# The first attention unit's scores and group maxima, moved from the attention stage into the value loop of the projection

## The reference

```
x = LN(x + attention(x));  x = LN(x + softmax(cross scores) * ...);  x = LN(x + mixture_of_experts(x))
```

```
q, k, v = x@Wq+bq, x@Wk+bk, x@Wv+bv          # split into 16 heads of 32
local:   query block i (128 rows) sees keys in [128 i - 64, 128 (i+1) + 64)
global:  row 0, row 511 and the 62 rows of largest |q| per head see all 512 keys
```

## Time and profile before

| | us |
|---|---|
| three executions | 1150.06, 1471.1, 1154.42 |
| median | 1154.42 |
| profiled execution | 1150.03 |
| its span, first to last instruction | 1148.3 |

### The profile page before, as it was taken

The page is one execution under the profiler, slowest core; times in us unless marked ns, Lnnn a source line. Parts: engine busy times, 40 slices in busy tenths (PEclk is TensorE's granted clock), DMA queues, the critical chain, the costliest instruction groups (busy, mean ns, idle before and its releaser), DMA issues. The chain is left out here.

```text
span 1148.3 us, 18035 instructions
## 1 busy us (share of the span) xinstructions
PE 983.3 (86%) x5111; PEld 710.3 (62%) x5111; DVE 761.1 (66%) x1328; ACT 612.8 (53%) x919; POOL 465.8 (41%) x423
## 2 busy tenths in 40 slices
PE   5999995899999999971899999992879999999940
PEld 4567884434444344420798989891868888888830
DVE  3325534877777677603888888853777888888925
ACT  4333210366767667642444444441667888888824
POOL 2000000154546455445566666623234555555424
PEclk9999998699999999985899999996899999999975
DMA  7454404443424334004211111123785444344327
GB/s 253 152 183 165 165 1 83 82 102 65 110 65 99 88 76 109 1 1 163 63 56 56 57 55 55 56 66 129 254 254 135 73 72 73 72 73 73 65 37 293
DMA packets 80881, 115.71 MB, mean 101 GB/s; under 512 B 15680, under 2 KB 37056, under 8 KB 80832
## 3 DMA queue, kind: packets, MB, share of 16 engines
q1 hardware_dynamic: 65648, 90.17, 27.0%
q0 software_dynamic: 9760, 20.49, 9.8%
q10 hardware_dynamic: 5424, 4.46, 1.2%
HBM read 74.77 MB, written 40.31 MB: 100 GB/s over the span
## 5 line engine op out<-in xcount | busy, mean ns | idle before, releaser
L718 DVE TENSOR_REDUCE maxima<-ps_s 128x8 f32<-128x512 f32 x256 | 168.7, 689 | 71.1 <-PE ps_s L586 69.4
L554 POOL TENSOR_TENSOR pair_sum<-probs 128x2048 f32<-128x2048 f32 x32 | 146.0, 4564 | 164.1 <-ACT probs L693 164.1
L1643 DVE TENSOR_TENSOR we_lo<-w_all,we_hi 128x1408 fp32r<-128x1408 f32 (+1 forms) x117 | 188.7, 1666 | 29.8 <-ACT we_hi L1583 24.4
L693 ACT ACTIVATE probs<-ps_st 128x512 f32<-128x512 f32 x256 | 146.4, 600 | 93.2 <-PE ps_st L635 89.6
L1583 ACT ACTIVATE we_hi<-w_all 128x1408 fp32r (+1 forms) x117 | 161.4, 1412 | 34.6 <-PE e_ps_y L1691 15.3
L586 PE MATMUL ps_s<-k,q 96*128 96x512 f32 x256 | 115.2, 458 | 14.9 <-DMA k<-qk_dram 11.9
L635 PE MATMUL ps_st<-q,k 128*128 128x512 f32 x256 | 121.0, 474 | 4.8 <-ACT probs L693 1.9
L1566 POOL DMA_INDIRECT x_dram<-e_y,who x39 | 64.1, 1644 | 131.7 <-ACT e_y L1600 118.4
L635 PEld LDWEIGHTS ps_st<-q,k 128*128 128x128 f32 x256 | 49.0, 192 | 109.5 <-ACT probs L693 77.1
L1560 POOL DMA_INDIRECT xg<-x_dram,who x39 | 74.3, 1905 | 43.1 <-DMA who<-table_dram 20.0
L1373 PE MATMUL ps_gu<-sw_hi,x2T_hi 128*128 128x352 f32 (+1 forms) x256 | 88.7, 346 | 1.8 <-issue 1.5
(11 more groups left out here) (241 smaller groups left out, 2392.2 us busy)
## 6 DMA issues: line engine op xcount, KB each, us to landing
qk_dram<-qk_ctx SPq DMA_DIRECT2D x32, 512.0 KB, 2.8
q<-qk_dram SPq DMA_DIRECT2D x96, 128.0 KB, 3.2
k<-qk_dram SPq DMA_DIRECT2D x96, 128.0 KB, 3.4
w_all<-in_L_ffn_w_gate_dram SPq DMA_DIRECT2D x8, 704.0 KB
w_all<-in_L_ffn_w_up_dram SPq DMA_DIRECT2D x8, 704.0 KB
x_dram<-x SPq DMA_DIRECT2D x16, 256.0 KB, 2.0
x_dram<-attn SPq DMA_DIRECT2D x16, 256.0 KB
w_all<-in_L_ffn_w_down_dram SPq DMA_DIRECT2D x8, 512.0 KB
```

The source lines that it names most:

```text
L554: pool.tensor_tensor(pair_sum[:, h], probs[:, 2 * h], probs[:, 2 * h + 1], ALU.add).then_inc(added, 1)
L693: act.activation(probs[:, kc, j, :], ps_st[:, s % 2, :], ACT.Exp, scale=SCALE).then_inc(exp_done, 1)
L718: dve.tensor_reduce(by_tile[:, t, j, 1:9], ps_s[:, x % 2, :].rearrange("p (g n) -> p g n", n=S // 8), axis=AX.X, op=ALU.max).then_inc(s_re ...
L1643: dve.tensor_tensor(w_lo[kind][:], raw(base, kind), w_hi[kind][:].bitcast(F32), ALU.subtract).then_inc(s[kinds[kind] + "_lo"], 1)
```

## The change

1. The loads of unit 0 are issued in `project`, on SP, after the store of part 19 (i = NQ + 3), into tensors `q_first` and `k_first` of their own. SP first waits there for the store of part 16, unit 0's keys. Their `window` rows are copied by DVE at i = 29 (4 copies). `attend` uses these two as its slot 0 and has memory of its own for the other two slots only.
2. In the value loop each tile n is followed by one score matmul of unit 0 (`first_score`), and DVE makes the group maxima of it right after the bias addition of that tile, before what else the tile has for it. The 16 tiles carry the 16 scores. Their PSUM bank is the one in which the norms were summed.
3. `attend` begins with unit 1's loads (24 loads ahead of the loop, not 36). DVE begins with `row_maxima(0)`, then 8 window copies, then the units. PE begins with `turn(0)` and goes into the steps of unit 0. The scores of unit 1 are no longer started ahead: in unit 0, two of them are issued in each of the steps s = 2 to 8, and one each at s = 9 and 10 (`scored_by`). From s = 11 on the order is the old one.
4. To make room, buffers of `project` become views of `c.v` (written by the value loop) and `c.attn`: the input rows, zeros, table entries, `head_cols`, context input, `work`, `bar`. The context's load waits for the split of Wq, and the first value tile waits for the stores of zeros and table (`rows_out`, `table_out`).
5. POOL clears `maxima` in `project`, not in `attend`.

```diff
+def unit_parts(q, k, qk_dram, u):
+    for half in range(2):
+        for r in range(3):
+            for tile, which, part in ((q, 0, r // 2), (k, 1, r % 2)):
+                src = qk_dram[which, part, bass.ds(u, 1), 2 * HD * half:2 * HD * (half + 1)]
+                yield (tile[HD * r:HD * (r + 1), 2 * half:2 * half + 2, :].bitcast(F32), ...)
...
 # project, SP
                     sp.dma_start(qk_dram[i // NQ, :, b * HG + g:b * HG + g + 1]...then_inc(parts_stored[i % 4], 16)
+                    if i == NQ + 3:
+                        sp.wait_ge(parts_stored[0], 16 * (NQ // 4 + 1))
+                        for dst, src in unit_parts(c.q_first, c.k_first, qk_dram, 0):
+                            sp.dma_start(dst, src).then_inc(first_in, 16)
 # project, DVE
+                    if i == NQ + 13:
+                        dve.wait_ge(window_done, 1)
+                        for j in range(HPG):
+                            dve.tensor_copy(c.k_first[BR:P, j, :], c.window[BR:P, :])
...
                         dve.tensor_tensor(c.v[...], ps_proj[...], bias_v[...], ALU.add).then_inc(v_out, 1)
+                        dve.wait_ge(first_scored, n + 1)
+                        if n == 0:
+                            dve.wait_ge(maxima_cleared, 1)
+                        dve.tensor_reduce(group_maxima(c.maxima, t, b), ps_first[:]...,
+                                          axis=AX.X, op=ALU.max).then_inc(first_reduced, 1)
 # project, PE
+                def first_score(n):
+                    j, t = divmod(n, TT)
+                    if n:
+                        pe.wait_ge(first_reduced, n)
+                    else:
+                        pe.wait_ge(first_in, NDMA)
+                        pe.wait_ge(step, 2)
+                    pe.matmul(ps_first[:], c.q_first[0:BR, j, t * P:(t + 1) * P], c.k_first[0:BR, j, :],
+                              start=True, stop=True).then_inc(first_scored, 1)
...
                     values(n)
                     if n % TT == 1:
                         c_part(n // TT)
+                    first_score(n)
 # attend, SP
-                for u in range(SLOTS):
+                for u in range(1, SLOTS):
                     load_unit(u, u, True)
 # attend, PE
+                def scored_by(s):
+                    return min(NU, s + 1 + EARLY, max(0, 2 * (s - 1)))
...
-                        if s < NU - EARLY and not last:
+                        if first:
+                            for x in range(scored_by(s - 1), scored_by(s)):
+                                score(1, 1, x, 0)
+                        elif s < NU - EARLY and not last:
                             score(u + 1, (p + 1) % SLOTS, s + EARLY, uses + (p + 1) // SLOTS)
...
-                pe.wait_ge(window_in, SLOTS * HPG)
+                pe.sem_inc(s_done, NU)
                 pe.wait_ge(cleared, 2)
-                for x in range(NU):
-                    score(0, 0, x, 0)
                 turn(0)
-                for x in range(EARLY):
-                    score(1, 1, x, 0)
+                pe.wait_ge(window_in, (SLOTS - 1) * HPG)
                 units(pe, unit)
 # attend, DVE
-                for p in range(SLOTS):
+                dve.sem_inc(s_reduced, NU)
+                dve.wait_ge(cleared, 1)
+                row_maxima(0)
+                for p in range(1, SLOTS):
                     for j in range(HPG):
-                        dve.tensor_copy(k4[BR:P, p, j, :], c.window[BR:P, :]).then_inc(window_in, 1)
-                dve.wait_ge(cleared, 1)
-                for x in range(NU):
-                    reduce(0, x)
-                row_maxima(0)
+                        dve.tensor_copy(k4[p][BR:P, j, :], c.window[BR:P, :]).then_inc(window_in, 1)
                 for x in range(EARLY):
                     reduce(1, x)
```

More of the change, by code:

```diff
@@ L62, with group_maxima @@
     pass
+def unit_parts(q, k, qk_dram, u):
[3 more added lines that the diff above has]
+                src = qk_dram[which, part, bass.ds(u, 1), 2 * HD * half:2 * HD * (half + 1)]
+                yield (tile[HD * r:HD * (r + 1), 2 * half:2 * half + 2, :].bitcast(F32),
+                       src.rearrange("a (j p) n -> p (a j) n", p=HD))
+def group_maxima(maxima, t, j):
+    return maxima[:, 0:TT * HPG * GW].rearrange("p (t j g) -> p t j g", j=HPG, g=GW)[:, t, j, 1:9]
 def project(nc, c, x, wq, bq, wk, bk, wv, bv, qk_dram, context, x_wq, x_bq, x_wk, x_bk, table_dram, x2_dram, x3_dram):
@@ L169, in _ @@
                             pool.wait_ge(built, n)
+                pool.sem_inc(window_done, 1)
+                pool.memset(c.maxima[:], -SENTINEL).then_inc(maxima_cleared, 1)
             @block.sync
@@ L181, in _ @@
                 for rows in (x2_dram, x3_dram):
-                    sp.dma_start(rows[T:T + P, :], zeros[:]).then_inc(rows_out, 16)
+                    sp.dma_start(rows[T:T + P, :], zeros).then_inc(rows_out, 16)
                 sp.dma_start(table_dram.rearrange("(p n) a -> p (n a)", p=P),
-                             no_token[:].rearrange("p n a -> p (n a)").bitcast(U32)).then_inc(table_out, 16)
+                             no_token.rearrange("p n a -> p (n a)").bitcast(U32)).then_inc(table_out, 16)
                 for i in range(2 * NQ):
@@ L298, in choose @@
                         dve.wait_ge(norm_acc, NQ)
-                        dve.tensor_copy(work[:, 0:S], ps_norm[:]).then_inc(step, 1)
+                        dve.tensor_copy(work[:, 0:S], ps_norm).then_inc(step, 1)
                     dve.wait_ge(step, 2 * r + 2)
-                    dve.max(top8[:], work[:]).then_inc(step, 1)
+                    dve.max(top8[:], work).then_inc(step, 1)
                     dve.wait_ge(step, 2 * r + 3)
-                    dve.match_replace(work[:], top8[:], work[:], -1.0).then_inc(step, 1)
+                    dve.match_replace(work, top8[:], work, -1.0).then_inc(step, 1)
                 def raise_bar():
@@ L307, in raise_bar @@
                     dve.wait_ge(step, n)
-                    dve.tensor_scalar(bar[:], work[:, 0:S], 0.0, NEG_SEL, ALU.is_ge, ALU.mult).then_inc(step, 1)
+                    dve.tensor_scalar(bar, work[:, 0:S], 0.0, NEG_SEL, ALU.is_ge, ALU.mult).then_inc(step, 1)
                     dve.wait_ge(step, n + 1)
@@ L483, in attend @@
         m = Memory(nc, ctx)
-        q4 = m.sb("q4", [P, SLOTS, HPG, S], F32R)
-        k4 = m.sb("k4", [P, SLOTS, HPG, S], F32R)
+        q_more = m.sb("q_more", [P, SLOTS - 1, HPG, S], F32R)
+        k_more = m.sb("k_more", [P, SLOTS - 1, HPG, S], F32R)
+        q4 = [c.q_first] + [q_more[:, p] for p in range(SLOTS - 1)]
+        k4 = [c.k_first] + [k_more[:, p] for p in range(SLOTS - 1)]
         vu = m.sb("vu", [P, TT, P])
@@ L493, in attend @@
         rsum = m.sb("rsum", [P, TT, HPG])
-        maxima = m.sb("maxima", [P, TT * (HPG * GW + 2)])
+        maxima = c.maxima
         m_all = m.sb("m_all", [P, TT, HPG])
@@ L540, in _ @@
                 pool.memset(turn_in[:], 0.0)
[L541 to L542 removed]
+                pool.memset(first_rows[:], 0.0).then_inc(cleared, 1)
                 pool.wait_ge(cleared, 1)
@@ L562, in load_unit @@
                         sp.wait_ge(st_done, NU * (u - SLOTS + 1))
[L563 to L566, removed]
-                                sp.dma_start(tile[HD * r:HD * (r + 1), p, 2 * k:2 * k + 2, :].bitcast(F32),
-                                             src.rearrange("a (j p) n -> p (a j) n", p=HD)).then_inc(unit_in[p], 16)
-                for u in range(SLOTS):
+                    for dst, src in unit_parts(q4[p], k4[p], qk_dram, u):
+                        sp.dma_start(dst, src).then_inc(unit_in[p], 16)
+                for u in range(1, SLOTS):
                     load_unit(u, u, True)
@@ L1836, in decoder @@
                 c.window = m3.sb("window", [P, S])
+                c.q_first = m3.sb("q_first", [P, HPG, S], F32R)[:]
+                c.k_first = m3.sb("k_first", [P, HPG, S], F32R)[:]
+                c.maxima = m3.sb("maxima", [P, TT * (HPG * GW + 2)])
                 c.bar = m3.sb("bar_kept", [P, TT, B * H])
```

61 lines of the change are left out of this document (35 added, 26 removed).

## The result

| | before | after |
|---|---|---|
| median of the executions, us | 1152.82 | 1141.84 |
| lowest and highest, us | 1150.06 to 1471.1 | 1140.33 to 1145.79 |
| profiled execution, us | 1150.03 | 1143.19 |
| its span, us | 1148.3 | 1141.4 |

The ratio after to before is 0.9912, interval 0.9891 to 0.9933: about 10 us of 1153, within 2%, as forecast (1140, range 1133 to 1150). The ratio is taken without the single execution at 1471.1 us, which stands alone. The profiled pair differs by 6.8 us only, so the first thing to read is where the other 3 us went.

The account below looks back on a forecast made before the run. Both stages run at PE's pace; between them PE waits for unit 0's loads, then scores at low clock. Gains of 8.4 to 13.4 us, taken as 11.0, from 1150.03 gave 1139.0; plus 1 for spread, 1140, range 1133 to 1150.

Parts of the forecast that it names:

- The score matmuls: Value loop, PE: unit 0's 16 scores add 3.6 us, at 0.223 us each.
- Rival A: Value loop and key half: score matmuls cost 0.39 us or more, or stores delay PE; gain only 3 to 8 us; chance 0.13.
- The reduces: Value loop, DVE: 16 reduces of 0.65 us, 15 hidden in idle time, the last adding 0.65 us.
- The loads in the key half: Key half, SP: unit 0's 12 load issues hold the queue 6.0 us but cost nothing, at most 0.4 us.
- The views in other memory add no operation: Projection buffers placed in other memory: no operation added, no cost counted.
- The window copies: Key half, DVE: four copies, 1.7 us between parts 29 and 30, fit in 1.97 us of idle time; cost nothing.
- The wait for unit 1's loads in the old place: Attention's start: PE waits 11.89 us for unit 1's loads instead of unit 0's; unit 1's first score at 202.8.
- Unit 1's scores: Unit 0's steps: paired scores put the 16th at 214.6 at low clock, 212.8 at full; gains 10.6 and 12.4 us.
- 16th score at 212 to 215: Sign that the forecast is right: unit 1's 16th score in attention starts at 212 to 215 us.
- Behind the mark: After unit 1's 16th score (225.24 before): low clock loses 2.2 us, or up to 0.95 us is saved behind `m_bar`.
- Rival B: Attention from unit 0's step 2: small gaps keep the clock at 0.50; 1157 us with one whole unit so; chance 0.07.

Follow-up runs that it names:

- aligned: The changed kernel with the tensor maxima at 1024 bytes per partition instead of 672; ratio to the kernel before 0.9929.
- kept_warm: The changed kernel with 15 additional matmuls, read by nothing, where PE waits at attention's start; 1143.88 us, ratio to the kernel before 0.9940.
- after_again: The changed kernel executed once more without an edit; 1142.35 us, ratio to the kernel before 0.9929.
- five_ahead: The changed kernel with five scores of unit 1 ahead of unit 0's first step, then one per step; 1145.52 us, ratio to the kernel before 0.9943.
- three_aligned_warm: The changed kernel with units 1 and 2 also loaded early, maxima at 1024 bytes, four unread matmuls before the first turn; 1136.5 us, ratio 0.9851.

## Why the prediction was right, step by step

**The score matmuls, 3.6 us:** 3.64 measured (51.50 - 47.86), 0.23 us a matmul. Rival A, with 0.39 us a matmul, is out. The first load did come 7.0 us later (189.03 to 196.02), the 7 us of rival A, but 2.7 of them by the start and the key half and not by its mechanism.

**The reduces, hidden but the last, 0.65:** the first load comes 3.00 us after the last bias addition, before 2.38: 0.62. That makes 4.3, as forecast.

**The loads in the key half, nothing:** right, by aligned; in the changed kernel ACT waited for PE alone from 90 to 139 us. One row was misread: 195.05 is the 14th load, the 12th stands at 194.12, so that an issue takes 0.47 us and not 0.50. In the changed kernel the 12 issues ran from 105.82 to 111.43. It changes nothing.

**"The views in other memory add no operation": the step that was wrong.** They add none, but I let that stand for no cost. The new tensors ahead of the projection's buffers moved these to addresses at which the matmuls of the key half, not those of the value loop, start further apart: +1.2 us (K 45.36 against 44.15, and 44.15 again in aligned).

**The window copies, nothing:** four took 1.44 us (133.52 to 134.96 in the changed kernel) between parts 29 and 30. Right.

**The wait for unit 1's loads in the old place:** right in its end (9.37 us from first issue to first score), wrong in its form. I had named one wait of 10 to 12 us for a load; it is three. The copies set unit 0's first step, at 201.50, 5.5 us behind the first load where the sum had 6.7 (193.3 to 200.0), and the three steps ahead of the load's end ran as forecast.

**Unit 1's scores:** forecast 11.8 us from the first to the 16th at the low clock, 9.95 or a little less at full; measured 12.07 at the low clock, in the 0.50 rows, and 9.59 in kept_warm with the clock at 1.00 (205.53 to 215.12). Both ends were priced right and I took the middle, 0.4 us above the low one; the low one came. The sign "16th score at 212 to 215" failed as it stands, 217.46; 2.7 us of that had come in before the value loop. Behind the mark the slow products (1.93 us against 1.07) lost 0.9, and the short `m_bar` (0.17 against 1.80) and the 0.95 us that PE had waited behind it gave that back; the two are not measured apart.

The sum for the profiled pair: +1.5 (start) + 1.2 + 3.6 + 0.6 + 0.1 until the first load; -14.8 from there to the 16th score (21.44 us against 36.21); -0.1 behind the mark: -7.9 at attention's last output (508.11 against 516.04 on DVE). The later stages took 1.1 us more in this execution: -6.8. Without the start and the later stages, which vary, the change is worth 9.4 us; forecast 11.0. The ratio says 10.1 with 7.7 to 12.6, that of after_again 8.2. The difference of 1.6 to the forecast is the 1.2 us of the key half and 0.4 for the low clock.

That 1141.84 came so near to 1140 is in part luck. The profiled execution was forecast at 1139.0 and took 1143.19; the start and the later stages made 2.6 of these 4.2 us, and the forecast had no term for them. The median then fell below the profiled execution, where I had added 1 us for the opposite.

**Rival B, the clock that stays low:** its place and condition were right for longer than I thought, from 201 to 220 us of the trace, but it ends once the matmuls start without gaps, from 217.03 on. The Trainium skill ("TensorE: Matmul & The Clock Gate", "The HAM clock gate") gives sustained work as what lifts the clock. By that rule, the traces agree: it is up at 205 in kept_warm, where PE was given work from 196.9 on, and in five_ahead before 215, against 220 in the changed kernel. With the four matmuls of three_aligned_warm, from 195.73 on, it did not rise earlier.

## What to carry to other kernels

A wait that a moved operation leaves behind belongs to the next one in the queue: here the load's wait went from unit 0 to unit 1, and only loading all three units early took it away (0.9866 against 0.9912; with the aligned size 0.9840 against 0.9929). A low-cost way to price such a change is to measure a distance inside the trace that starts behind what varies. And when buffers move, compare the mean of the same matmuls before and after: here 672 bytes in front of the moving operand, and not of the weights, put the starts 3% further apart.

## What the runs showed of the hardware that I had not expected

Back-to-back fp32r matmuls of 512 columns in the key half started 0.227 us apart (three in 0.68 us) in the kernel before and in aligned, where the turned inputs, their moving operand, lie a multiple of 1024 bytes further on. They started 0.234 us apart with the inputs 672 bytes off that place. K was 44.15, 45.36 and, at 704 bytes, 45.20 us. The key weights lie ahead of the new tensors and did not move. In the value loop and in the query half weights and moving operand moved together, and neither changed: the value loop took 51.50 us in the changed kernel and 51.43 in aligned, and parts 3 to 15 took 53.6 us before, in the changed kernel and in aligned. Whether the distance between the two operands or the address of one matters, and which multiple is enough, was not tried.
